# A causal attention, a second attention and a mixture of experts on one core: masked tiles spread between full ones, shorter DVE chains, start-up loads on two queues, and a last block whose expert rows return by products with ones

## What is computed

```python
# first layer: causal attention with rotary positions, 16 heads of width 8
Q, K, V = rope(x @ Wq.T), rope(x @ Wk.T), x @ Wv.T
x = layernorm(x + (softmax(causal(Q @ K.T / sqrt(8))) @ V) @ Wo.T)
# second layer: attention without a mask, then a top-1 mixture of 8 experts
y = x + msa(layernorm(x, ln1_w, ln1_b), w_qkv, w_proj)
h = layernorm(y, ln2_w, ln2_b)
e = argmax(h @ gate_w + gate_b)                  # one expert for each token
y = y + gelu(h @ w1[e], approximate=True) @ w2[e]   # 128 -> 512 -> 128
x = layernorm(x + y)
```

## Time and profile before

| what | us |
|---|---|
| three runs of the kernel | 893.73, 896.61, 900.15 |
| median | 896.61 |
| the profiled execution's own time | 894.7 |
| its span, first to last instruction | 893.0 |

### The profile page before, as it was taken

One profiled execution on the slowest core, in us unless ns is written; L12 is line 12 of the kernel. 1 busy time (PEld: TensorE's weight loads), 2 busy tenths in 40 slices (PEclk: granted clock), 3 DMA queues, 4 the chain that ended last, 5 costly groups with the idle time before them and its releaser, 6 DMA issues.

```text
span 893.0 us, 24266 instructions
## 1 busy us (share of the span) xinstructions
PE 809.2 (91%) x9940; PEld 369.5 (41%) x9952; DVE 328.5 (37%) x948; ACT 775.7 (87%) x906; POOL 228.5 (26%) x367
## 2 busy tenths in 40 slices
PE   8689999999999998999999999999999999996271
PEld 4244444444443443444344444444444444443240
DVE  5434525312430014320042433255332363334763
ACT  3579889999999998999999999999999899994440
POOL 5542211111110010000003343323334141443382
PEclk9799999999999999999999999999999999998575
DMA  8977220202110431810201000301000010001001
GB/s 273 269 210 224 96 49 2 95 2 49 49 48 1 108 84 40 244 50 3 48 2 32 1 3 3 78 8 37 3 3 19 14 43 3 1 3 31 30 14 41
DMA packets 34644, 51.60 MB, mean 58 GB/s; under 512 B 4064, under 2 KB 15072, under 8 KB 34528
## 3 DMA queue, kind: packets, MB, share of 16 engines
q1 hardware_dynamic: 32992, 46.30, 18.2%
q0 software_dynamic: 1536, 3.67, 1.3%
HBM read 29.12 MB, written 20.84 MB: 56 GB/s over the span
## 4 chain that ended last, share of the span: by engine, by line
PE 76%; DVE 8%; ACT 4%; issue 4%; DMA 2%; SPq 2%; POOL 2%; POOLq 1%; another core or an unknown queue 1%; DVEq 0%; ACTq 0%
PE ps L488 72%; ACT probs L922 3%; PE ps L493 3%; PE ps L787 1%; POOLq L1070 1%; DMA query_rows<-q_scratch 1%; POOL parts L1077 1%; DVE ln_newton L1156 1%; DMA q_scratch<-parts 1%; DVE q_rotated L1312 1%; DVE ln_newton L1155 1%; DVE z_rows L1176 1%; DVE ln_stats L1161 0%; DVE ln_newton L1154 0%
## 5 line engine op out<-in xcount | busy, mean ns | idle before, releaser
L922 ACT ACTIVATE probs<-ps 128x1024 f32<-128x1024 f32 (+3 forms) x832 | 736.0, 1017 | 41.5 <-PE ps L488 35.1
L488 PE MATMUL ps<-probs,values 128*9 128x256 f32 (+1 forms) x6528 | 426.3, 374 | 4.7 <-DVE q_rotated L1312 3.1
L488 PE MATMUL ps<-query_rows,key_rows 32*128 32x512 f32 (+3 forms) x1664 | 282.5, 485 | 17.5 <-ACT probs L922 10.2
L488 PEld LDWEIGHTS ps<-probs,values 128*9 128x9 f32 x6528 | 143.3, 90 | 182.5 <-issue 94.4
L488 PEld LDWEIGHTS ps<-query_rows,key_rows 32*128 32x128 f32 x1664 | 117.3, 183 | 183.5 <-issue 93.1
L1043 POOL TENSOR_SCALAR_AFFINE_SELECT probs<-probs 128x256 f32<-128x256 f32 x128 | 53.0, 420 | 234.4 <-ACT probs L922 231.5
L1090 POOL COPY parts<-early_late 128x512 f32 x63 | 44.5, 744 | 124.6 <-PE ps L488 124.6
L1048 POOL DMA_INDIRECT z_sorted<-z_rows,slot_numbers x16 | 15.8, 988 | 218.3 <-DVE slot_numbers L1447 208.8
L1312 DVE COPY q_rotated<-ps 128x512 f32<-128x512 f32 x30 | 20.7, 690 | 124.7 <-PE ps L488 124.6
L1077 POOL COPY parts<-parts 128x512 f32 x72 | 44.9, 663 | 29.3 <-PE ps L488 28.8
L1324 DVE RECIPROCAL recip<-ps 128x16 f32<-128x16 f32 x32 | 8.2, 256 | 70.5 <-PE ps L493 65.1
(11 more groups left out here) (184 smaller groups left out, 586.4 us busy)
## 6 DMA issues: line engine op xcount, KB each, us to landing
k_scratch<-parts SPq DMA_DIRECT2D x16, 512.0 KB, 3.9
q_scratch<-parts SPq DMA_DIRECT2D x16, 512.0 KB, 5.5
query_rows<-q_scratch SPq DMA_DIRECT2D x32, 256.0 KB, 5.3
key_rows<-k_scratch SPq DMA_DIRECT2D x20, 256.0 KB, 4.6
key_rows<-k_scratch SPq DMA_DIRECT2D x16, 192.0 KB, 4.5
parts<-in_w SPq DMA_DIRECT2D x1, 2048.0 KB, 8.9
early_late<-in_w SPq DMA_DIRECT2D x8, 256.0 KB, 8.0
early_late<-z_sorted SPq DMA_DIRECT2D x4, 384.0 KB, 3.1
```

The costliest lines, as they stand in the source:

```text
L488: return nc.tensor.matmul(out, l, r, start=start, stop=stop, skip_group_check=True)
L922: nc.scalar.activation(Pr[:, t % KEPT, 2 * p:2 * p + 2, lo:BLK], score_banks(t, p)[:, :, lo:BLK], ACT.Exp, bias=-SHIFT[r["a"]], scale=SCAL ...
```

## The change

1. **Order of masked tiles.** In layer 1, blocks 1 to 3, masked tiles lie between full ones.
2. **Start-up.** 16 loads go from SP's queue to ACT's. Keys are written to DRAM once and read with each part twice. The rows of the first group of heads are asked for first, those of groups 1 to 3 after them (keys of one group at a time). PE waits for the first group alone before its first run. DVE rotates block 0 before it waits for two small constants.
3. **Roots.** The first Newton turn is replaced by a cubic one of 4 chained instructions, and one Newton turn follows instead of two, in every layernorm and in the second root of `rows_to_h`. There the last turn comes after `due(PREP_AT[b][0] - 1)`, which is 13, 13, 13, 12 for b = 0 to 3, instead of `due(13)`.
4. **Routing.** Maximum and one-hot come from two reductions and three multiplications or comparisons over all 4 tiles at once; the running sums take three chained steps instead of four and one copy.
5. **Gathers of blocks 0 and 1** start at steps 4, 6, 8, 10 of the block two later, instead of 1, 2, 3, 4.
6. **Block 3's return.** No store and no gathers. SP loads place numbers (`places`, 128 x 774 numbers, in a new step `places_in` on its queue) once the last sums are taken. After block 2's layernorm DVE writes diagonals of `dest` (4 instructions 128x128); PE multiplies them with ones, which gives every token's place in every partition (128x512 in PSUM); DVE compares that with the place numbers, 6 instructions of 128x512; PE sums 4 products 128x128x128 for each round into one bank, before the next round's down product and once at the end; DVE adds the bank to x and does a whole layernorm.

```diff
+ORDER = (
+    (0, 1, 2, 3),
+    (0, 1, 2, 3, 6, 4, 7, 5),
+    (0, 1, 2, 3, 4, 5, 11, 6, 10, 7, 9, 8),
+    (0, 1, 2, 3, 4, 5, 6, 7, 8, 15, 9, 14, 10, 13, 11, 12),
+)
...
-            causal, kt = r["a"] == 1, r["k0"] + n
+            causal = r["a"] == 1
+            order = ORDER[r["qb"]] if causal else range(r["k0"], r["k1"])
+            kt = order[n]
...
             def keys_out(a, b):
                 sp.wait_ge(A[a]["k_split"], b + 1)
-                for i in range(NP):
-                    sp.dma_start(k_scratch[a - 1, i, :, :, :, b * BLK:(b + 1) * BLK].rearrange("j d h t -> (d h) j t"),
-                                 k3[:, b]).then_inc(k_out[b], 16)
+                sp.dma_start(k_scratch[a - 1, :, :, :, b * BLK:(b + 1) * BLK].rearrange("j d h t -> (d h) j t"),
+                             k3[:, b]).then_inc(k_out[b], 16)
...
+            def first_rows():
+                sp.wait_ge(k_out[0], 16)
+                key_rows_in(1, 0, 1, 0, BLK, k_first)
+                sp.wait_ge(q_out[0], 32)
+                query_rows_in(1, 0, 0, 1, q_first)
+                for g in range(1, G):
+                    key_rows_in(1, g, g + 1, 0, BLK, k_rows[0])
+                query_rows_in(1, 0, 1, G, q_rows[0])
...
+            nc.scalar.dma_start(wa[:, 2 * D:4 * D], wa_d[:, 2 * D:4 * D]).then_inc(ld_a, 16)
+            for w in (slice(0, 2 * D), slice(4 * D, 5 * D)):
+                nc.scalar.dma_start(wa[:, w], wa_d[:, w]).then_inc(ld_q, 16)
+            for t, s in ((blkf, blk_d), (ident, ident_d)):
+                nc.scalar.dma_start(t[:, :], s).then_inc(ld_w, 16)
             act.wait_ge(dch, 1)
             nc.scalar.activation(gen_rec[:, :], onesf[:, 0:1], ACT.Exp)
+            for t, s in ((wo, wo_d), (wqkv, wqkv_d), (wproj, wproj_d), (gw, gw_d), (iota, iota_d), (gb, gb_d)):
+                nc.scalar.dma_start(t[:, :], s).then_inc(ld_e, 16)
...
+            def cubic(y, c, t, u):
+                link(tt(t, y, y, ALU.mult))
+                link(tt(t, t, c, ALU.mult))
+                link(nc.vector.scalar_tensor_tensor(out=u, in0=t, scalar=-1.25 / CUBIC, in1=t, op0=ALU.add, op1=ALU.mult))
+                link(nc.vector.scalar_tensor_tensor(out=y, in0=u, scalar=1.875, in1=y, op0=ALU.add, op1=ALU.mult))
...
-                        pace(first_step(2, b + 2) + 1 + i)
+                        pace(first_step(2, b + 2) + 4 + 2 * i)
...
-                due(13)
+                cubic(y, c, t, u)
+                due(PREP_AT[b][0] - 1)
...
+                link(nc.vector.tensor_reduce(mx, lg[:, :, :], AX.X, ALU.max))
+                link(tt(oh[:, :, :], lg[:, :, :], mx.unsqueeze(2).to_broadcast([P, TB, E]), ALU.is_equal))
+                link(tt(lg[:, :, :], oh[:, :, :], first_wins[:, :].unsqueeze(1).to_broadcast([P, TB, E]), ALU.mult))
...
+            def m_dest_rows():
+                pe.wait_ge(m_diag, 1)
+                mm(ps[:, 0, :], onesf[:, :], att[:, :, :].rearrange("p i d -> p (i d)")).then_inc(m_row, 1)
+            def m_sum(r):
+                pe.wait_ge(m_taken, taken(b, "down", r))
+                pe.wait_ge(m_at, r + 1)
+                for i in range(TB):
+                    last = mm(ps[:, 1, i * P:(i + 1) * P], ones_at[r].bitcast(F32)[:, i * P:(i + 1) * P], yS[:, r, :],
+                              r == i == 0, r == ROUNDS - 1)
             for k, (_, name, r) in enumerate(AT_END):
+                if name == "down" and r:
+                    m_sum(r - 1)
                 side_op[name](b, k, r)
+                if (name, r) == ("sorted", 1):
+                    m_dest_rows()
+            m_sum(ROUNDS - 1)
...
+            def dest_diag():
+                for i in range(TB):
+                    ins = ts(att[:, i, :], ident[:, :], destf[:, i:i + 1], None, ALU.mult)
+                ins.then_inc(m_diag, 1)
+            def ones_of(rounds):
+                dve.wait_ge(ld_n, 16)
+                dve.wait_ge(m_row, 1)
+                for r in rounds:
+                    ts(ones_at[r], ps[:, 0, :], place_of[:, r:r + 1], None, ALU.is_equal).then_inc(m_at, 1)
...
+            dest_diag()
             experts(b, AT_END, at_once)
-            for i in range(TB):
-                row = xn[:, b * TB + i, :]
-                dve.wait_ge(m_tile[i], 16)
-                link(tt(row, row, yback[:, i, :], ALU.add))
-                last = nc.vector.bn_stats(st[:, i, :], row)
-            link(last)
             xb = xn[:, b * TB:(b + 1) * TB, :]
-            normalize(xb, xb).then_inc(m_out, 1)
+            dve.wait_ge(m_summed, 1)
+            link(tt(xb, xb, ps[:, 1, :].rearrange("p (i d) -> p i d", i=TB), ALU.add))
+            layernorm(xb, xb).then_inc(m_out, 1)
```

More of the change, by code:

```diff
@@ L38 @@
 THETA = 10000.0
+CUBIC = float(np.sqrt(3.0 / 8.0))
 P = 128
@@ L341, in build @@
         kaf, qaf = KAv.bitcast(F32), QAv.bitcast(F32)
+        ones_at = [(KAv[:, 3, r * BLK:(r + 1) * BLK] if r < 4 else KAv[:, r - 3, S - BLK:S]) for r in range(ROUNDS)]
+        given_places = Pr[:, KEPT - 1].rearrange("p h t -> p (h t)")[:, 0:SORTED + ROUNDS]
+        places, place_of = given_places[:, 0:SORTED], given_places[:, SORTED:SORTED + ROUNDS]
         values_of = {1: V, 2: V2}
@@ L349, in run_step @@
         def run_step(r, n):
-            causal, kt = r["a"] == 1, r["k0"] + n
+            causal = r["a"] == 1
+            order = ORDER[r["qb"]] if causal else range(r["k0"], r["k1"])
+            kt = order[n]
             cut = causal and kt >= r["qb"] * TB
-            done = sum(TB for q in RUNS[:r["n"]] if q["a"] == 1)
+            done = r["n"] * TB + sum(k >= r["qb"] * TB for k in order[:n])
             return dict(r=r, t=r["t0"] + n, kt=kt, lo=(kt % TB) * P if cut else 0,
-                        cut=2 * (done + kt % TB) + 1 if cut else None, start=n == 0, stop=kt == r["k1"] - 1)
+                        cut=2 * done + 1 if cut else None, start=n == 0, stop=n == len(order) - 1)
         block = ctx.enter_context(nc.Block())
@@ L395, in first_key_rows, with query_rows_in @@
-            def first_key_rows(b):
-                sp.wait_ge(k_out[b], 32)
-                rows_in(kaf[:, :, b * BLK:(b + 1) * BLK], k_scratch, 1, 0, G, b * BLK, (b + 1) * BLK, k_rows[b])
+                    sp.dma_start(kaf[f * ROWS:(f + 1) * ROWS, g0:g1, t0:t1],
+                                 src[f, :, g0:g1, t0:t1].unsqueeze(0).to_broadcast([NP, NP * DK, g1 - g0, t1 - t0])).then_inc(done, 16)
+            def query_rows_in(a, b, g0, g1, done):
+                src = q_scratch[a - 1].rearrange("i j d (g f) t -> f (i j d) g t", f=HG)
+                for f in range(HG):
+                    sp.dma_start(qaf[f * ROWS:(f + 1) * ROWS, b % 2, g0:g1],
+                                 src[f, :, g0:g1, b * BLK:(b + 1) * BLK]).then_inc(done, 16)
@@ L1118, in _ @@
                 for r in runs_in(1, qb):
-                    for i in range(TB):
-                        cut(run_step(r, qb * TB + i))
+                    for n, kt in enumerate(ORDER[qb]):
+                        if kt >= qb * TB:
+                            cut(run_step(r, n))
                     if r["n"] == 0:
@@ L1169, in normalize @@
                 link(ins)
-                v, y, h, t = (nw[:, n, :] for n in range(4))
+                v, y, h, t, c, u = (nw[:, n, :] for n in range(6))
                 link(ts(v, mv[:, :, 1], EPS, None, ALU.add))
-                rsqrt(y, v, h, t, 1)
+                root_start(y, h, c, mv[:, :, 1], v)
+                cubic(y, c, t, u)
                 between()
-                newton(y, h, t, 2)
+                newton(y, h, t, 1)
                 for i in range(TB):
@@ L1486, in experts @@
                         mark(ts(c, side[:, 0:c.shape[1]], ln[:, 2:3], ln[:, 3:4], ALU.mult, ALU.add), m_taken, n)
+                        if b == NB - 1 and r == 1:
+                            ones_of(range(ROUNDS))
                     elif name == "up":
@@ L1573, in _ @@
             dve.wait_ge(ld_e, 16 * 10)
+            ts(first_wins[:, :], iota[:, :], -1.0, float(E), ALU.mult, ALU.add)
             dve.wait_ge(init, 3)
@@ L1635 @@
             (p[:, None] // ROWS == np.arange(HG)[None, :]).astype(np.float32)], axis=1),
+        places=np.concatenate([np.tile(np.arange(SORTED), (P, 1)), p[:, None] + P * np.arange(ROUNDS)[None, :]],
+                              axis=1).astype(np.float32),
     )
```

122 lines of the change are left out of this document (63 added, 59 removed).

## The result

| what | us |
|---|---|
| changed kernel, 4 runs | 969.87 to 973.37, median 971.47 |
| kernel before, 4 runs beside it | 891.32 to 900.15, median 895.17 |
| ratio, 95% interval | 1.085 [1.079, 1.091] |
| the profiled execution and its span | 969.87, 967.7 |

The kernel became 76 us slower, where a gain of 19 us was forecast and 887 was the upper end of the range.

What follows compares the result with a forecast made beforehand. ACT (87% busy) and PE (91%) were taken to bound the middle, gains lying where one rests. Gains 3.1 + 6.0 + 2.3 + 1.1 + 0.5 + 5.8 = 18.8 us gave a median of 878 us, range 868 to 887.

Steps and rivals of the forecast that it cites:

- term 1: Start-up and x's load: first scores 5.5 us earlier, 2.4 lost again in block 1 waiting for x; -3.1 us.
- the rival that the new row loads take as long as was saved: Start-up: source read twice and quarter pieces use up the saving, x stays where it was; 881 us, 7%.
- Whatever the start wins, block 1 goes on when x is there: Layer 1, block 1: the residual add waits for x, so 2.4 of 5.5 us won are lost again.
- Term 2: Layer 1, blocks 1 to 3: masked tiles between full ones remove ACT's idle between runs; 1.3, 2.2, 2.5; -6.0 us.
- The rival of a wait at every masked tile: Layer 1: each spread masked tile has the 0.76 us wait, +27.4 instead of -6.0; 911 us, 4%.
- Term 3: Start of layer 2: last root turn and z before the copied sums remove ACT's 2.29 us idle; -2.3 us.
- Terms 4 and 5: Layer 2: shorter layernorm roots in three blocks, -1.1 us; later, wider-spread gathers, -0.5 us.
- Term 5: Gathers in layer 2: later ones may avoid ACT's 1.45 us stop or move it; -0.5, between -1.5 and +1.5.
- Term 6: The end: routing and root -1.4, diagonals +0.5, comparisons +0.8, sums +1.3, tail -7.0; together -5.8 us.
- diagonals and comparisons: The end, on DVE: diagonals +0.5 us (0 to 2.7), comparisons +0.8 us (0 to 4.1).
- five sums: The end: PE sums before down products cost +1.3 us; bounds -1.3 (PE keeps high clock) to 9.4.
- the rule weighed in the prediction: The end: DVE and GpSimd lock one port pair per instruction; diagonals could wait for POOL's copies, costing over 0.5 us.

Runs made afterwards that it cites:

- experiment 4: Kernel with each key load cut into two plain 16-row loads, plus small timed probe loads of six forms: 3.94 us with 2 copies outermost, 1.79 for 32 plain rows.
- written_twice: Changed kernel with the previous kernel's key path (keys written twice, read once as plain rows): 884.15 us, ratio 0.986.
- before_x_early: Kernel before the change, with block 0's part of x alone asked for right behind the second query rows: 893.30 us, ratio 1.000.
- before_repeat: Kernel before the change with only the changed key path (written once, read with the repeated dimension outermost): 985.65 us, ratio 1.099.
- two_plain: Changed kernel, keys still written once, each key load cut into two plain loads of 16 rows: 893.99 us, ratio 0.997.
- experiments 5 and 6: Block 0's x asked for early, behind the second query rows: in written_twice 875.10 us; in the kernel before the change 893.30 us.
- natural_order: written_twice with the old order of key tiles in layer 1's blocks 1 to 3 (masked tiles last): 888.82 us, ratio 0.992.
- experiment 10: combined with the gathers of layer 2's first blocks back at the old steps 1 to 4: 879.67 us (2 runs), ratio 0.981.
- combined: written_twice with block 0's x asked for early and the five first loads back on SP's queue: 873.47 us, ratio 0.978.

## Why the prediction was wrong

**The step that failed** is the costing of the key loads within term 1: each was priced at 0.62 us by a row of four plain query loads, and the only doubt was the rival that the new row loads take as long as was saved, at 7% and 881. The row's loads had 32 rows outermost, the new ones 2. They cost 2.5 us each where they queue up (10.02 for four), 86 us in all (967.7 against 881.6). The rival had the right place and a bound that was far too near: it let the new form lose what the write had saved and no more. A form of transfer that no row of the trace shows needed an upper end worked out from its own shape, and the page of the Trainium skill named in experiment 4 has the rule for it.

**Term 1 without that** (-3.1) came out at +4.3 in written_twice: the start -3.1, block 0 +0.5, and block 1 +6.9. Two things were wrong in it. The first scores were won by less (30.48 instead of the forecast's 27.8, and 28.9 to 30.8 in the traces of all kernels with the new start): PE waits for no rows any more, but it has projections of its own until then, and it began them 0.84 later (5.18 against 4.34). What the positions freed on SP's queue are worth is not shown: its first key write is issued at 15.72, against 15.80 before, but this place moves from one execution to the next (14.14 to 16.06 in the others with the new start, 15.21 and 16.19 in before_x_early and before_repeat). And x landed 2.2 later (79.87 against 77.72). The 3.1 that the forecast had it earlier came from the single write, which written_twice gives up; in no kernel could that be read by itself, for in the changed kernel and in two_plain slower or more numerous loads stand ahead of x. "Whatever the start wins, block 1 goes on when x is there" was half right: it does so only once x is later than the first run's end (experiments 5 and 6).

**Term 2, masked tiles** (-6.0): right in size. Against natural_order blocks 2 and 3 gave 2.0 and 3.1 (forecast 2.2 and 2.5). With x early block 1 gave 1.0 (1.3), but only against the kernel before, which lacks the rest of the change too, so that part is argued; together 6.1. Against the kernel before, blocks 2 and 3 show 1.8 and 1.9 only: the old order costs 0.2 and 1.2 more in the changed kernel than it did there, of which one ACT wait of 0.84 in block 3's first run is natural_order's alone. The mechanism is nearly as forecast: in runs without side work the 0.76 between runs is gone, but 0.42 is left inside, so not nearly all of it went. The rival of a wait at every masked tile falls.

**Term 3, start of layer 2** (-2.3): right. The block takes 119.25 in written_twice, 2.2 less than before; the 2.29 of the earlier trace rows is gone. No experiment took this edit out alone.

**Terms 4 and 5, roots and gathers** (-1.1 and -0.5): together -3.2 (blocks 1 to 3 of layer 2, -0.5, -1.1, -1.6). The stops of 1.16 and 1.45 us in blocks 2 and 3 went with the pace of the gathers (experiment 10). before_x_early has the old roots and no stops, and its three blocks are longer than written_twice's by 0.5, 0.4 and 0.0: some 0.9 for the roots (PE's wait for z rows in these blocks fell from 0.58 to 0.26 or 0.27), which leaves 2.3 for term 5 instead of 0.5. Term 5 was mis-sized, because its row was taken as a wait that later gathers may only move.

**Term 6, the end** (-5.8): -6.5 in the changed kernel, and by its parts nearly so. Rows of its end:

```profile
911.21 0.19 DVE L1495 TENSOR_TENSOR logits<-ps,gate_b 128x32 f32<-128x32 f32 x1 [1.44 <-PE ps L517]
...
912.92 0.16 DVE L1508 TENSOR_TENSOR row_low<-row_low 128x8 f32<-128x8 f32 x1
...
921.80 5.07 DVE L1257 TENSOR_SCALAR x_rows<-x_rows,ln_meanvar,ln_newton 128x128 f32<-128x128 f32 x4
...
923.99 2.28 POOL L1154 COPY values<-early_late 128x512 f32 x4
...
926.25 1.54 PE L799 MATMUL ps<-ident,early_late 128*128 128x128 f32 x6 [12.05 <-DMA early_late<-z_sorted]
926.79 0.86 DVE L1578 TENSOR_SCALAR attn_rows<-ident,row_low 128x128 f32<-128x128 f32 x4
...
927.70 2.07 PE L517 MATMUL ps<-attn_rows,ones_f 128*128 128x512 f32 x2
...
929.91 4.04 DVE L1586 TENSOR_SCALAR key_rows<-ps,probs 128x512 fp32r<-128x512 f32 x6 [0.97 <-PE ps L517]
933.87 0.99 DVE L1537 SCALAR_TENSOR_TENSOR squares_blockdiag<-squares_blockdiag,early_late 128x512 f32<-128x512 f32 x1
...
958.26 0.29 DVE L1573 TENSOR_SCALAR early_late<-ps 128x128 f32<-128x128 f32 x1 [1.36 <-PE ps L517]
959.87 0.69 DVE L1684 TENSOR_TENSOR x_rows<-x_rows,ps 128x512 f32<-128x512 f32 x1 [1.32 <-PE ps L517]
...
961.50 0.38 DVE L1248 BATCH_NORM_AGGREGATE ln_meanvar<-ln_stats 128x2 f32<-128x6 f32 x4
```

Routing takes 1.9 us (911.21 to 913.08) against 2.95: -1.1 (forecast -1.0). From the end of the last result (958.55) to the aggregation are 2.95 us, where the earlier trace rows had 10.17: -7.2 (forecast -6.6). From PE's first transposes of sorted rows to the first GELU instruction are 7.62 us (926.25 to 933.87), 5.96 before (846.35 to 852.31): +1.7, where +1.3 was forecast for diagonals and comparisons. Its parts are others: PE's product that makes the rows took 2.07 and did not lie in PE's wait for DVE, where the forecast had put it; behind it the first up products begin 3.46 after the transposes (929.71), 2.78 before. That is 0.7. The other 1.0 is the comparisons, behind which the first GELU instruction starts without a wait; the diagonals gave nothing. From there to the last result 24.4 us against 23.7: +0.7 for five sums (+1.3). PE's clock was higher, as one end of that bound had it: in the first rounds (from 3.3 us ahead of the first GELU instruction) it was granted 0.89 of full speed, 0.70 in the same stretch before (849.04 to 864.40). How much of the term that gave is not shown.

```profile
930.60:946.00 15.40, 10.70 (x157) 6.61 (x150) 11.99 (x19) 6.77 (x13) 10.19 (x15) 0.89 0.01 1
```

Of the rule weighed in the prediction (the Trainium skill, "SBUF — State Buffer", section "SBUF: two separate sides") the trace bears out the first half: the scaling, 1.11 us alone, took 5.07 beside POOL's copies and ended 0.6 after the last of them (926.27). The diagonals behind it (from 926.79) found POOL idle and took 0.22 each, so they cost less, not more, than the 0.5 of the forecast. Neither set anything back, since DVE had slack there.

**In balance**, terms 2 to 6 were 15.7 in the forecast, and by the stretches of written_twice against before they are 15.6 (3.6 in blocks 2 and 3 of layer 1, 2.2, 3.2, 6.6), with block 1's part of term 2 hidden behind x. That the sums agree is in part luck: term 5 gave 1.8 more than forecast, and term 2 shows 2.4 less there. Term 1 turned from -3.1 into +4.3, which leaves the 11.4, and the key loads then cost 86. With before's key path and x early, the kernel takes 873.47 to 875.10, 20 to 21 us less than the kernel before beside it. That is about what was forecast, but not a confirmation of it: the early x is no part of the change.

**Not shown:** keys written once and read with 16 rows outermost and the copies inside, in the kernel itself. A kernel with that form for block 0 of layer 1 (combined_once, expected within 1 us of combined) gave no time. By the probes the form should be near the plain one and save half of the key writes; that is argued.

## What to carry to other kernels

Before a transfer's shape is changed, look at the first dimension of both its sides: bytes and issue count can be the same while the number of DMA engines that carry it falls from 16 to 2. A price taken from a trace row holds for the form in that row alone; where an edit changes the form, the upper end of its cost must come from the new form. And a wait shown in a row costs only what it keeps from the bounding engine: test by an early load whether it costs anything, since here 4.82 us of it were free and 9.74 cost 7.9.

## What the runs showed of the hardware

- Loads with an outermost count of 2 took 3.74 to 3.94 us for 64 KB alone, against 1.76 to 1.79 with 32; queued four in a row at 256 KB they took 10.0 us against 2.5. In the slow form two packets of 2 KB were under way together, in the plain one up to 16.
- A load that reads its source twice, rows outermost, costs 0.5 to 0.8 us more than 32 plain rows (2.28 and 2.58), near what two separate loads cost (2.23).
- At the last of four indirect gathers issued 1.3 us apart by POOL, ACT stopped for 1.2 to 2.2 us, and DVE and PE beside it, in three of four traces, and no row explains it; with the gathers 2.9 to 4.2 us apart the stop did not appear in any of the nine traces that had that pace.
- Beside POOL's copies, four scalings of 128x128 on DVE took 5.07 us instead of 1.11 and ended just behind the last copy.
